# Splitting the first two context tiles of the next batch on ScalarE and VectorE as well as on GpSimd

## The chip, the cores and the metric

The kernel runs on one core of one Trainium2 chip. The metric is the device time of one execution in microseconds (us). Lower is better. The core has TensorE (matmuls; PE in the profile, its weight loads PEld), VectorE (DVE), ScalarE (ACT), GpSimd (POOL) and SyncE (SP), which here issues transfers. The engines run on their own and wait for each other through semaphores; each takes its instructions strictly in the order in which they are written.

## The reference, cut to what matters

The program is a chain of six layers on x (8 batches of 64 rows, 512 wide). The first is a cross attention to a context of 1601 rows per batch, with 32 query heads that share 8 heads of keys and values:

```python
q = (query @ Wq + bq).reshape(B, L, NKV, G, HDIM)       # 8, 64, 8, 4, 128
k_, v_ = jnp.split(kv @ Wkv + bkv, 2, axis=-1)          # kv: 8 x 1601 x 512
scores = jnp.einsum('blkgd,bmkd->bkglm', q, k) * scale
attn = jax.nn.softmax(scores, axis=-1)
o = jnp.einsum('bkglm,bmkd->blkgd', attn, v)
```

Behind it come a state space layer, a ternary linear layer, a second attention to the context, a self attention and a gated feed-forward layer. The change touches only the first attention.

## The kernel before

**The split.** TensorE's matmuls work on rounded operands (fp32r). To keep precision each operand is held as a high part (the value rounded by a copy) and a low part (the raw value minus the high part, the residue), and a product is three matmuls: high by high, high by low, low by high (the helper `product`, L59 to L61). So every operand must be split before TensorE can use it.

**The context.** For a batch the context lies in SBUF transposed, with the 512 features as four chunks of 128 partitions by 1602 columns, as `ctx_hi` and `ctx_lo`. It is loaded and split in four tiles (TILES) of 402, 402, 402 and 396 columns, so a tile is 128 partitions by 4 x 402 = 1608 elements. Raw tiles come into `ctx_raw`, which has two slots: tiles 0 and 2 share one, tiles 1 and 3 the other. `Context.split` does one tile on GpSimd: L110 the high part, L114 the low part (L109 and L113 do one padding column of the last tile). `hi_set` and `lo_set` count the tiles done; in the attention they are `ctx_hi_set` and `ctx_lo_set`.

**The work of one head** (index j = 0 to 7 in batch b). TensorE computes the scores against the key tiles that it made before (`scores`), the key tiles of the next head (`key_tile`, four tiles, 12 matmuls each), the attention of the head before (`attend`) and, after every even head, the values of this head and the next (`value_tile`, six tiles g = 0 to 5 of 256 context rows, 24 matmuls each). Key and value tiles go through `kv_ps`, two banks of PSUM in turn: ScalarE copies the high part out, VectorE then makes the residue (L855, L862) and counts `kv_free`, and the tile after the next may begin. ScalarE also copies the scores out, does the exponentials and the high parts of the probabilities; VectorE the maxima, the shifts and the sums; GpSimd the low parts of the probabilities (`low`, L504, L508, L511), the split of one row of sums (`sum_low`, L533, L536) and of the weights and queries that come next.

**The change of batch** comes seven times. In group j = 6 (NKV - 2) TensorE makes the last value tiles from the old context, and GpSimd, after `low` and `sum_low` of head 6, runs `split_ctx`: for each tile it waits until it has landed and until the value tiles that read the same columns are done, and splits it. Then follow the weights. SyncE loads the raw tiles 0 and 1 of the next batch long before, at j = 2. Tiles 2 and 3 it loads in group j = 6, each when the low part of the tile in the same slot is done:

```python
if j == NKV - 2 and not last:
    for t in range(2, NT):
        sp.wait_ge(ctx_lo_set, b * NT + NT + t - 1)
        context.load(sp, b + 1, t)
```

TensorE, in group j = 7, computes scores and attention and then the key tiles of head 0 of the next batch; there each key tile t waits for the low part of context tile t:

```python
if j % NKV == 0:
    at = b + j // NKV
    pe.wait_ge(ctx_lo_set, at * NT + t + 1)
```

The order on each engine is written out by hand in its `group` function, below. `drive` runs the groups of all heads and batches.

Of the kernel before, what the change touches and what calls it, by code (L numbers as in the profile page):

```python
# [7 lines left out]
F32 = mybir.dt.float32  # L8
F32R = mybir.dt.float32r
ACT = mybir.ActivationFunctionType  # L10
AX_X = mybir.AxisListType.X
AX_XY = mybir.AxisListType.XY
P = 128
# [37 lines left out]
def apart(eng, passed):  # L51


    eng.sem_inc(passed, 1)
# [214 lines left out]
def cross_attention(nc, context, early, rest, output, s_ps, st, wk, wv, ident, q_dram, o_dram):  # L269

    B, _, KC, S = context.ctx_t.shape
# [28 lines left out]
    def value_at(j):  # L300

        return key_at(j - j % 2) + 2 * NT
# [15 lines left out]
    def has_keys(j, last):  # L318

        return not (last and j == NKV - 1)  # L320

    with Scope(nc, "xa") as sc:
# [62 lines left out]
        def d_ps(j, alone=False):  # L385
            if alone:
                return m_ps[:, 0, :]
            return o_ps[:, j % 2, NQ:2 * NQ]

        def free_before(b, j, g):  # L390

            if g < NSLOT:
                return unit(b, j) * NG + (NSLOT, 1, 2)[g]
            return unit(b, j) * NG + g + 1
# [72 lines left out]
        def _(pool):  # L467
# [23 lines left out]

            def split_ctx(b, n):

                for t, (c, w) in enumerate(TILES):
                    pool.wait_ge(ctx_in[t], (n + 1) * 16)
                    used = min(NV, -(-(c + w) // (2 * P)))
                    pool.wait_ge(kv_full, b * KV_TILES + value_at(NKV - 2) + used)
                    apart(pool, passed)
                    context.split(pool, t, n * NT + t + 1)

# [214 lines left out]
        @block.scalar  # L715
        def _(act):
            def key_tile(b, j, t):
                c, w = TILES[t]
                n = key_at(j) + t
                act.wait_ge(kv_full, b * KV_TILES + n + 1)  # L720
                nc.scalar.activation(k_hi[:, c:c + w], kv_ps[:, n % 2, 0:w], ACT.Identity,  # L721
                                     bias=bk_sb[:, j % NKV:j % NKV + 1]).then_inc(kv_hi, 1)

            def value_tile(b, j, g):
                n = value_at(j) + g
                act.wait_ge(kv_full, b * KV_TILES + n + 1)
                nc.scalar.activation(v_hi[:, 2 * g:2 * g + 2, :], kv_ps[:, n % 2, :].rearrange("p (c d) -> p c d", c=2),  # L727
                                     ACT.Copy).then_inc(kv_hi, 1)

            def copies(b, j, start, until):  # L730
                for g in range(start, until):
                    m = min(2, NC - 2 * g)
                    r = rows(2 * g)
                    act.wait_ge(s_full, unit(b, j) * NG + g + 1)
                    nc.scalar.activation(st[0:r, j % 2, g, :, 0:m].rearrange("p q c -> p c q"),  # L735
                                         s_ps[0:r, g % NSLOT, 0:m * NQ].rearrange("p (c q) -> p c q", c=m),
                                         ACT.Copy).then_inc(s_free, 1)

            def diagonal(b, j):
                act.wait_ge(nmx_set, unit(b, j) + 1)  # L740
                for u in range(NU):
                    end = nc.scalar.activation(diag[:, u * P:(u + 1) * P], ident[:, :], ACT.Copy, scale=nmx[:, u:u + 1])
                end.then_inc(diag_set, 1)

            def exponential(b, j, p):
                t = scored(j, p)
                act.wait_ge(sub_set, unit(b, j) * NP + p + 1)
                nc.scalar.activation(t, t, ACT.Exp, scale=SCALE).then_inc(exp_set, 1)  # L748

            def high(b, j, p):  # L750
                act.wait_ge(exp_set, unit(b, j) * NP + p + 1)
                act.wait_ge(o_full, unit(b, j) + 1)
                if p == NP - 1:
                    nc.scalar.activation(pt_rest[0:ROWS, :, :],
                                         rest_scores(j, 0, ROWS).unsqueeze(1).broadcast_to([ROWS, 2, NQ]),
                                         ACT.Copy).then_inc(hi_set, 1)
                    return
                nc.scalar.activation(by_chunk(pt_hi, p), scored(j, p).rearrange("p g q c -> p g c q"),  # L758
                                     ACT.Copy).then_inc(hi_set, 1)

            def upper_sums(b, j):
                act.wait_ge(sum_set, unit(b, j) + 1)
                nc.scalar.activation(upper[:, :], sums[HP:P, 1, :], ACT.Copy).then_inc(upper_set, 1)

            def with_bias(b, j):
                act.wait_ge(on_set, unit(b, j) + 3)
                nc.scalar.activation(o_sb[:, j % 2], o_sb[:, j % 2], ACT.Identity,
                                     bias=bv_sb[:, j:j + 1]).then_inc(o_free, 1)

            def first():  # L770
                act.wait_ge(bias_in, 32)
                for t in range(NT):
                    key_tile(0, 0, t)
                group(0, 0, False, True)

            def first_unit(b, j):

                exponential(b, j, 0)
                exponential(b, j, 1)
                value_tile(b, j, 0)  # L780
                exponential(b, j, 2)
                exponential(b, j, 3)
                high(b, j, 0)
                value_tile(b, j, 1)
                high(b, j, 1)
                high(b, j, 2)
                value_tile(b, j, 2)
                high(b, j, 3)
                upper_sums(b, j)
                for g in range(3, NV):  # L790
                    value_tile(b, j, g)

            def group(b, j, last, alone=False):
                if j % 2 == 0:
                    copies(b, j, 0, NG)
                    if not alone:
                        high(b, j - 1, 0)
                        upper_sums(b, j - 1)
                    key_tile(b, j + 1, 0)
                    if not alone:  # L800
                        high(b, j - 1, 1)
                    key_tile(b, j + 1, 1)
                    if not alone:
                        high(b, j - 1, 2)
                        high(b, j - 1, 3)
                    key_tile(b, j + 1, 2)
                    diagonal(b, j)
                    key_tile(b, j + 1, 3)
                    if alone:
                        first_unit(b, j)  # L810
                        return
                    for p in range(NP):
                        exponential(b, j, p)
                    high(b, j, 0)
                    high(b, j, 1)
                    value_tile(b, j, 0)
                    with_bias(b, j - 1)
                    high(b, j, 2)
                    high(b, j, 3)
                    for g in range(1, NV):  # L820
                        value_tile(b, j, g)
                        if g == 2:
                            upper_sums(b, j)
                elif has_keys(j, last):
                    copies(b, j, 0, NG)
                    diagonal(b, j)
                    key_tile(b, j + 1, 0)
                    with_bias(b, j - 1)
                    exponential(b, j, 0)
                    key_tile(b, j + 1, 1)  # L830
                    exponential(b, j, 1)
                    key_tile(b, j + 1, 2)
                    exponential(b, j, 2)
                    exponential(b, j, 3)
                    key_tile(b, j + 1, 3)
                else:
                    copies(b, j, 0, NG)
                    diagonal(b, j)
                    for p in range(NP):
                        exponential(b, j, p)  # L840
                        high(b, j, p)
                    upper_sums(b, j)
                    act.wait_ge(kv_full, B * KV_TILES)
                    output.second_high(act)
                    with_bias(b, j - 1)

            drive(act, first, group, lambda b: with_bias(b, NKV - 1))

        @block.vector
        def _(dve):  # L850
# [59 lines left out]
            def summed_in_two(b, j, h):  # L910
# [6 lines left out]
                else:  # L917
# [4 lines left out]
                    nc.vector.tensor_tensor(sums[:, 1, :], sums[:, 0, :], m_ps[:, 1, :], ALU.add).then_inc(sum_main, 1)  # L922
                    with_rest(b, j)

            def folded(b, j):
                dve.wait_ge(upper_set, unit(b, j) + 1)
                nc.vector.tensor_tensor(upper[:, :], sums[0:HP, 1, :], upper[:, :], ALU.add).then_inc(fold_set, 1)
# [33 lines left out]
            def group(b, j, last, alone=False):  # L961
                if j % 2 == 0:
# [20 lines left out]
                    for g in range(2, NV):  # L983
                        value_tile(b, j, g)
                        if g == 2:
                            folded(b, j)
                    return
                maxima(b, j, 0)
                maxima(b, j, 1)
# [2673 lines left out]
```

## Time and profile before

| | |
|---|---|
| median of 3 runs | 2604.21 us (2603.81 to 2615.51) |
| profiled execution | 2602.36 us |
| its span, from the first to the last instruction | 2600.6 us |
| TensorE matmuls busy | 2480.7 us |
| VectorE busy | 1844.5 us |
| ScalarE busy | 1503.5 us |
| GpSimd busy | 1499.0 us |
| mean granted clock of TensorE, as a share of full speed | 0.982 |

The first attention takes the stretch from about 130 to 1870 us. "Busy" counts the time in which an instruction ran. A wait is put down to the instruction whose end released it. Times in a timeline are microseconds from the start of the span.

### The profile page before, as it was taken

The numbers are of one execution on the slowest core, as the hardware profiler recorded it, in microseconds if no ns is written. First come the engines' busy times: TensorE is split into PE (matmuls) and PEld (weight loads), VectorE is DVE, ScalarE is ACT, GpSimd is POOL, SyncE is SP. The second block draws the span as 40 slices with busy tenths as digits, with TensorE's granted clock in tenths as the row PEclk, the third lists the DMA queues.
The fourth block names the chain that finished last, engine by engine and source line by source line (L and its number), as shares of the span: only waits on it lengthen the run. The fifth ranks groups of instructions, "written<-read, shape, count | busy, mean of one in ns | idle before, by whom it ended". The sixth has DMA issues, their size and how long they took to land. (4 is left out here: it accounts for less than half of the span.)

```text
span 2600.6 us, 42754 instructions
## 1 busy us (share of the span) xinstructions
PE 2480.7 (95%) x16984; PEld 2271.7 (87%) x16984; DVE 1844.5 (71%) x2078; ACT 1503.5 (58%) x2591; POOL 1499.0 (58%) x1222
## 2 busy tenths in 40 slices
PE   8999999999999999999999999999999699989889
PEld 6899999999999999999999999999977477754557
DVE  4158777778777787777877777777756699843473
ACT  3356656666665666556665566666643577622672
POOL 3345696586668569657666855966510499400352
PEclk9999999999999999999999999999999799999889
DMA  6511111121101201102110121110261300188200
GB/s 222 191 59 54 30 59 54 35 66 54 37 22 60 73 29 60 55 29 65 62 31 28 60 66 35 54 37 28 74 217 53 130 1 1 53 295 310 97 1 17
DMA packets 112239, 188.72 MB, mean 73 GB/s; under 512 B 9940, under 2 KB 74836, under 8 KB 110252
## 3 DMA queue, kind: packets, MB, share of 16 engines
q1 hardware_dynamic: 103724, 177.64, 20.4%
q10 hardware_dynamic: 8320, 8.39, 0.9%
q8 instruction: 133, 2.18, 0.4%
q14 instruction: 62, 0.51, 0.1%
HBM read 165.98 MB, written 20.02 MB: 72 GB/s over the span
## 5 line engine op out<-in xcount | busy, mean ns | idle before, releaser
L504 POOL TENSOR_TENSOR xa_pt_lo<-xs_st,xa_pt_hi 128x1024 fp32r<-128x1024 f32 x191 | 468.2, 2480 | 454.4 <-ACT xa_pt_hi L758 454.4
L59 PE MATMUL ctx_kv_ps<-ctx_wv_hi,ctx_hi 128*128 128x256 f32 x1536 | 431.7, 281 | 1.8 <-DVE xa_v_lo L862 1.8
L60 PE MATMUL ctx_kv_ps<-ctx_wv_lo,ctx_hi 128*128 128x256 f32 x1536 | 430.0, 280 | 0.0
L61 PE MATMUL ctx_kv_ps<-ctx_wv_hi,ctx_lo 128*128 128x256 f32 x1536 | 429.9, 280 | 0.0
L59 PE MATMUL ctx_kv_ps<-ctx_hi,ctx_wk_hi 128*128 128x402 f32 (+1 forms) x1024 | 360.1, 352 | 21.2 <-POOL ctx_lo L114 19.4
L60 PE MATMUL ctx_kv_ps<-ctx_lo,ctx_wk_hi 128*128 128x402 f32 (+1 forms) x1024 | 354.2, 346 | 0.0
L61 PE MATMUL ctx_kv_ps<-ctx_hi,ctx_wk_lo 128*128 128x402 f32 (+1 forms) x1024 | 354.2, 346 | 0.0
L59 PEld LDWEIGHTS ctx_kv_ps<-ctx_wv_hi,ctx_hi 128*128 128x128 f32 x1536 | 288.6, 188 | 2.2 <-DVE xa_v_lo L862 2.2
L60 PEld LDWEIGHTS ctx_kv_ps<-ctx_wv_lo,ctx_hi 128*128 128x128 f32 x1536 | 289.4, 188 | 0.0
L61 PEld LDWEIGHTS ctx_kv_ps<-ctx_wv_hi,ctx_lo 128*128 128x128 f32 x1536 | 288.5, 188 | 0.0
L735 ACT ACTIVATE xs_st<-xs_s_ps 128x512 f32<-128x512 f32 (+1 forms) x448 | 262.9, 603 | 29.5
L748 ACT ACTIVATE xs_st<-xs_st 128x1024 f32<-128x1024 f32 (+1 forms) x256 | 228.1, 903 | 64.8 <-DVE xs_st L896 56.7
L896 DVE TENSOR_TENSOR xs_st<-xs_st,xa_m_ps 128x1024 f32<-128x1024 f32 (+1 forms) x256 | 253.8, 1013 | 5.9 <-PE xa_m_ps L635 2.7
L727 ACT ACTIVATE xa_v_hi<-ctx_kv_ps 128x512 fp32r<-128x512 f32 x192 | 114.8, 598 | 245.2 <-PE ctx_kv_ps L61 245.2
L855 DVE SCALAR_TENSOR_TENSOR xa_k_lo<-ctx_kv_ps,ctx_bk_sb,xa_k_hi 128x402 fp32r<-128x402 f32 (+1 forms) x256 | 161.9, 633 | 123.7 <-ACT xa_k_hi L721 123.7
L862 DVE TENSOR_TENSOR xa_v_lo<-ctx_kv_ps,xa_v_hi 128x512 fp32r<-128x512 f32 x192 | 131.8, 686 | 158.0 <-ACT xa_v_hi L727 158.0
L721 ACT ACTIVATE xa_k_hi<-ctx_kv_ps,ctx_bk_sb 128x402 fp32r<-128x402 f32 (+1 forms) x256 | 152.5, 596 | 156.8 <-PE ctx_kv_ps L61 149.8
L61 PE MATMUL xs_s_ps<-xa_q_hi,xa_k_lo 128*128 128x256 f32 (+1 forms) x832 | 234.7, 282 | 0.0
L59 PE MATMUL xs_s_ps<-xa_q_hi,xa_k_hi 128*128 128x256 f32 (+1 forms) x832 | 233.6, 281 | 0.0
L60 PE MATMUL xs_s_ps<-xa_q_lo,xa_k_hi 128*128 128x256 f32 (+1 forms) x832 | 233.1, 280 | 0.0
L867 DVE TENSOR_REDUCE xa_m_ps<-xs_st 128x256 f32<-128x1536 f32 (+1 forms) x97 | 188.2, 1940 | 53.0 <-ACT xs_st L735 48.9
L59 PE MATMUL xa_o_ps<-xa_pt_hi,xa_v_hi 128*128 128x256 f32 x768 | 216.9, 282 | 0.8 <-DVE xa_pt_lo L931 0.8
(528 smaller groups left out, 6761.9 us busy)
## 6 DMA issues: line engine op xcount, KB each, us to landing
ctx_raw<-in_ctx_t SPq DMA_DIRECT2D x24, 804.0 KB, 6.7
ctx_wk_raw<-in_xa_wk SPq DMA_DIRECT2D x64, 256.0 KB, 2.8
ctx_wv_raw<-in_xa_wv SPq DMA_DIRECT2D x32, 512.0 KB, 4.3
n_back<-in_ctx SPq DMA_DIRECT2D x8, 1280.0 KB, 10.3
q_raw<-in_xa_wq SPq DMA_DIRECT2D x8, 1024.0 KB, 5.0
q_scratch<-q_q_sb ACTq DMA_DIRECT2D x8, 1024.0 KB, 4.4
ctx_q_raw<-q_scratch SPq DMA_DIRECT2D x64, 128.0 KB, 2.7
o_scratch<-xa_o_sb SPq DMA_DIRECT2D x64, 128.0 KB, 1.7
```

The source lines that it names most:

```text
L59: nc.tensor.matmul(out, left[0], right[0], start=first, stop=False)
L60: nc.tensor.matmul(out, left[0], right[1], start=False, stop=False)
L61: return nc.tensor.matmul(out, left[1], right[0], start=False, stop=last)
L504: nc.gpsimd.tensor_tensor(by_chunk(pt_lo, p), scored(j, p).rearrange("p g q c -> p g c q"), by_chunk(pt_hi, p).bitcast(F32), ALU.subtract) ...
L721: nc.scalar.activation(k_hi[:, c:c + w], kv_ps[:, n % 2, 0:w], ACT.Identity, bias=bk_sb[:, j % NKV:j % NKV + 1]).then_inc(kv_hi, 1)
L727: nc.scalar.activation(v_hi[:, 2 * g:2 * g + 2, :], kv_ps[:, n % 2, :].rearrange("p (c d) -> p c d", c=2), ACT.Copy).then_inc(kv_hi, 1)
L735: nc.scalar.activation(st[0:r, j % 2, g, :, 0:m].rearrange("p q c -> p c q"), s_ps[0:r, g % NSLOT, 0:m * NQ].rearrange("p (c q) -> p c q", ...
L748: nc.scalar.activation(t, t, ACT.Exp, scale=SCALE).then_inc(exp_set, 1)
L855: nc.vector.scalar_tensor_tensor(out=k_lo[:, c:c + w], in0=kv_ps[:, n % 2, 0:w], scalar=bk_sb[:, j % NKV:j % NKV + 1], in1=k_hi[:, c:c + w ...
L862: nc.vector.tensor_tensor(v_lo[:, 2 * g:2 * g + 2, :], kv_ps[:, n % 2, :].rearrange("p (c d) -> p c d", c=2), v_hi[:, 2 * g:2 * g + 2, :]. ...
L867: return nc.vector.tensor_reduce(out, st[:, j % 2, a:z, :, :].rearrange("p g q c -> p q g c"), AX_XY, op)
L896: nc.vector.tensor_tensor(t, t, m_ps[0:r, 1, :].unsqueeze(1).unsqueeze(3).broadcast_to([r, g, q, m]), ALU.add).then_inc(sub_set, 1)
```

## The change

At a change of batch, the split of tiles 2 and 3 stays as it was, and the steps of tiles 0 and 1 are shared out. ScalarE makes the high part of tile 0 after value tile 2 (and the copy of the upper sums), and the high part of tile 1 after value tile 4. VectorE makes the low part of tile 0 after value tile 3. GpSimd makes the low part of tile 1 as the first step of `split_ctx`, when both high parts and the low part of tile 0 are done, and then splits tiles 2 and 3 as before. The waits for the value tiles that read the same columns go with the high parts. The loads and what they wait for are not changed.

```diff
--- before.py
+++ after.py
@@ -386,6 +386,11 @@
             if alone:
                 return m_ps[:, 0, :]
             return o_ps[:, j % 2, NQ:2 * NQ]
+
+        def values_used(b, t):
+
+            c, w = TILES[t]
+            return b * KV_TILES + value_at(NKV - 2) + min(NV, -(-(c + w) // (2 * P)))
 
         def free_before(b, j, g):
 
@@ -491,10 +496,14 @@
 
             def split_ctx(b, n):
 
-                for t, (c, w) in enumerate(TILES):
+                pool.wait_ge(ctx_hi_set, n * NT + 2)
+                pool.wait_ge(ctx_lo_set, n * NT + 1)
+                apart(pool, passed)
+                raw, hi, lo = context.parts(1)
+                nc.gpsimd.tensor_tensor(lo, raw, hi.bitcast(F32), ALU.subtract).then_inc(ctx_lo_set, 1)
+                for t in range(2, NT):
                     pool.wait_ge(ctx_in[t], (n + 1) * 16)
-                    used = min(NV, -(-(c + w) // (2 * P)))
-                    pool.wait_ge(kv_full, b * KV_TILES + value_at(NKV - 2) + used)
+                    pool.wait_ge(kv_full, values_used(b, t))
                     apart(pool, passed)
                     context.split(pool, t, n * NT + t + 1)
 
@@ -757,6 +766,13 @@
                     return
                 nc.scalar.activation(by_chunk(pt_hi, p), scored(j, p).rearrange("p g q c -> p g c q"),
                                      ACT.Copy).then_inc(hi_set, 1)
+
+            def context_high(b, t):
+                n = b + 1
+                act.wait_ge(ctx_in[t], (n + 1) * 16)
+                act.wait_ge(kv_full, values_used(b, t))
+                raw, hi, _ = context.parts(t)
+                nc.scalar.activation(hi, raw, ACT.Copy).then_inc(ctx_hi_set, 1)
 
             def upper_sums(b, j):
                 act.wait_ge(sum_set, unit(b, j) + 1)
@@ -821,6 +837,8 @@
                         value_tile(b, j, g)
                         if g == 2:
                             upper_sums(b, j)
+                        if j == NKV - 2 and not last and g in (2, 4):
+                            context_high(b, g // 2 - 1)
                 elif has_keys(j, last):
                     copies(b, j, 0, NG)
                     diagonal(b, j)
@@ -921,6 +939,11 @@
                         dve.wait_ge(sum_lo_set, n)
                     nc.vector.tensor_tensor(sums[:, 1, :], sums[:, 0, :], m_ps[:, 1, :], ALU.add).then_inc(sum_main, 1)
                     with_rest(b, j)
+
+            def context_low(b, t):
+                dve.wait_ge(ctx_hi_set, (b + 1) * NT + t + 1)
+                raw, hi, lo = context.parts(t)
+                nc.vector.tensor_tensor(lo, raw, hi.bitcast(F32), ALU.subtract).then_inc(ctx_lo_set, 1)
 
             def folded(b, j):
                 dve.wait_ge(upper_set, unit(b, j) + 1)
@@ -984,6 +1007,8 @@
                         value_tile(b, j, g)
                         if g == 2:
                             folded(b, j)
+                        if j == NKV - 2 and not last and g == 3:
+                            context_low(b, 0)
                     return
                 maxima(b, j, 0)
                 maxima(b, j, 1)
```

## Rows read from the trace of the kernel before

**Rows 1.** The page: busy time, share of the span and instructions of the engines.
```profile
PE 2480.7 (95%) x16984; PEld 2271.7 (87%) x16984; DVE 1844.5 (71%) x2078; ACT 1503.5 (58%) x2591; POOL 1499.0 (58%) x1222
```

**Rows 2.** Who TensorE waited for, 130 to 1870 us: total, times, longest.
```profile
PE ctx_kv_ps L59 <- POOL ctx_lo L114: 19.4, 14, 2.4
```

**Rows 3.** Timeline of GpSimd, L533 once per head: start, us, instruction.
```profile
226.35 0.40 POOL L533 TENSOR_SCALAR xa_sum_halves<-xa_upper 64x256 fp32r<-64x256 f32 x1
...
280.16 0.40 POOL L533 TENSOR_SCALAR xa_sum_halves<-xa_upper 64x256 fp32r<-64x256 f32 x1
...
333.93 0.40 POOL L533 TENSOR_SCALAR xa_sum_halves<-xa_upper 64x256 fp32r<-64x256 f32 x1
...
392.37 0.40 POOL L533 TENSOR_SCALAR xa_sum_halves<-xa_upper 64x256 fp32r<-64x256 f32 x1
...
1757.06 0.40 POOL L533 TENSOR_SCALAR xa_sum_halves<-xa_upper 64x256 fp32r<-64x256 f32 x1
```

**Rows 4.** Timeline of GpSimd around the first change of batch.
```profile
324.69 7.44 POOL L504 TENSOR_TENSOR xa_pt_lo<-xs_st,xa_pt_hi 128x1024 fp32r<-128x1024 f32 x3
...
334.42 0.73 POOL L536 TENSOR_TENSOR xa_sum_halves<-xa_upper,xa_sum_halves 64x256 fp32r<-64x256 f32 x1
...
335.37 1.54 POOL L110 TENSOR_SCALAR ctx_hi<-ctx_raw 128x1608 fp32r<-128x1608 f32 x1 [0.23 <-POOL xa_sum_halves L536]
...
337.00 3.68 POOL L114 TENSOR_TENSOR ctx_lo<-ctx_raw,ctx_hi 128x1608 fp32r<-128x1608 f32 x1
...
345.71 1.53 POOL L110 TENSOR_SCALAR ctx_hi<-ctx_raw 128x1608 fp32r<-128x1608 f32 x1 [0.42 <-DMA ctx_raw<-in_ctx_t]
...
352.88 2.98 POOL L114 TENSOR_TENSOR ctx_lo<-ctx_raw,ctx_hi 128x1580 fp32r<-128x1580 f32 x1
```

**Rows 5.** Timeline of SyncE's queue: the two loads of tiles 2 and 3 merged.
```profile
340.70 5.20 SPq L93 DMA_DIRECT2D ctx_raw<-in_ctx_t  x2
```

**Rows 6.** Timeline of TensorE around the first change, single matmuls.
```profile
333.76 0.28 PE L59 MATMUL ctx_kv_ps<-ctx_wv_hi,ctx_hi 128*128 128x256 f32 x1
...
341.20 0.28 PE L59 MATMUL xa_o_ps<-xa_pt_hi,xa_v_hi 128*128 128x256 f32 x1
...
348.40 0.35 PE L59 MATMUL ctx_kv_ps<-ctx_hi,ctx_wk_hi 128*128 128x402 f32 x1
...
350.44 0.35 PE L61 MATMUL ctx_kv_ps<-ctx_hi,ctx_wk_lo 128*128 128x402 f32 x1
...
355.92 0.70 PE L59 MATMUL ctx_kv_ps<-ctx_hi,ctx_wk_hi 128*128 128x396 f32 x1 [2.41 <-POOL ctx_lo L114]
```

**Rows 7.** Busy times, 356 to 360 us; behind POOL: granted clock, DMA share.
```profile
356.00:360.00 4.00, 4.00 (x15) 4.00 (x16) 0.00 (x0) 0.14 (x1) 3.83 (x3) 0.60 0.02 4
```

**Rows 8.** Groups of ScalarE by shape, SBUF to SBUF: busy us, mean ns.
```profile
L1643 ACT ACTIVATE mp_w_hi<-ahead_raw 128x1024 fp32r<-128x1024 f32 x7 | 7.4, 1052 | 2.5 <-POOL mp_xpad L1586 2.5
...
L1345 ACT ACTIVATE q_w_hi<-q_raw 128x2048 fp32r<-128x2048 f32 x7 | 13.4, 1918 | 9.9 <-DMA v_scratch<-q_q_sb 5.5 <-ACT q_q_sb L1318 4.4
```

**Rows 9.** Groups of VectorE by shape, two SBUF inputs: busy us, mean ns.
```profile
L1696 DVE TENSOR_TENSOR mp_w_lo<-ahead_raw,mp_w_hi 128x1024 fp32r<-128x1024 f32 x7 | 8.6, 1222 | 3.7 <-ACT mp_w_hi L1643 3.7
...
L1375 DVE TENSOR_TENSOR q_w_lo<-q_raw,q_w_hi 128x2048 fp32r<-128x2048 f32 x7 | 17.8, 2538 | 54.3 <-ACT q_w_hi L1345 54.3
```

**Rows 10.** Timeline of ScalarE in the value tiles of head 6.
```profile
329.87 0.42 ACT L763 ACTIVATE xa_upper<-xa_sums 64x256 f32<-64x256 f32 x1 [0.96 <-DVE xa_sums L901]
...
333.96 0.60 ACT L727 ACTIVATE xa_v_hi<-ctx_kv_ps 128x512 fp32r<-128x512 f32 x1 [2.23 <-PE ctx_kv_ps L61]
```

**Rows 11.** Timeline of VectorE in the value tiles of head 6.
```profile
330.36 2.05 DVE L927 TENSOR_TENSOR xa_upper<-xa_sums,xa_upper 64x256 f32<-64x256 f32 x1
...
332.34 0.67 DVE L862 TENSOR_TENSOR xa_v_lo<-ctx_kv_ps,xa_v_hi 128x512 fp32r<-128x512 f32 x1
```

**Rows 12.** Spread of the fold (ns), and of the loads of the context.
```profile
L927 DVE TENSOR_TENSOR xa_upper<-xa_sums,xa_upper x64: 403/1432/2066, 169.3 to 1890.6; 64x256 f32<-64x256 f32 x64
...
DMA to landing us min/median/max: 4.8/6.2/11.7
```

## The prediction

> **What bounds the kernel now.** I read four views, in this order. First the page's busy times: TensorE's matmuls are busy for 95% of the span [rows 1], so a change to other engines can save only time in which TensorE stands still, or runs at a lower clock. Second, who TensorE waited for, in the stretch of the first attention: the largest sum there is 14 waits on the low part of a context tile, 19.4 us [rows 2]. There are seven changes of batch, so each has two such waits. Third, how long a pair of heads lasts. The reader is to take one GpSimd instruction that comes once per head, L533, as a clock: a pair inside a batch takes 280.16 - 226.35 = 53.81 us, the pair across the first change of batch 392.37 - 333.93 = 58.44 [rows 3]. From 226.35 to 1757.06 there are 28 pairs, seven of them across a change: 1530.71 - 28 x 53.80 (53.81 rounded down to the mean of several pairs) = 24.3 us is what all seven cost beyond their work, and it is the most that this change can give back there. The first costs 4.6, the other six 19.7 together, 3.3 each. Fourth, the timelines around the first change, to see what is late.
>
> The late thing is a chain, not GpSimd's load. The split of tile 2 needs a raw buffer that tile 0 frees. GpSimd starts tile 0 at 335.37, when it has finished head 6, and ends its low part at 340.68 (337.00 + 3.68); SyncE issues the load of tile 2 at 340.70 [rows 4, 5]. It has landed when GpSimd goes on at 345.71, 5.0 us later. High and low of tiles 2 and 3 then take until 352.88 + 2.98 = 355.86. So the last low part comes 15.16 us after that load is issued, and TensorE's key tile 3 starts at 355.92 [rows 4, 6]. Without the waits: tile 1 starts at 348.40, its twelfth matmul at 350.44, so twelve take 2.22 us and tiles 2 and 3 could start at 350.62 and 352.84 [rows 6]. Tile 3's lateness is 3.0 us; the small wait on tile 2 is inside it. At the first change TensorE then ran at a granted clock of 0.60 as a mean over 4 us, between the levels of 1.2 and 2.4 GHz, after standing still [rows 7]; that is the 4.6 against 3.3.
>
> **The change part by part.** ScalarE gets two copies of 128x1608. Rows of the same kind take 1052 ns at 1024 columns and 1918 at 2048 [rows 8]; in proportion between them, 1.55 us. VectorE gets one subtraction of two SBUF tiles: 1222 ns at 1024 and 2538 at 2048 [rows 9], so 1.97 us. The bounds are the rows at either size. GpSimd loses two high parts and one low part, 1.5 + 3.7 + 1.5 us. No transfer is added; two are issued at other times.
>
> *High part of tile 0.* It stands behind the upper sums, which end at 329.87 + 0.42 = 330.29 [rows 10]. So it runs 330.3 to 331.9. Its raw data was loaded four heads earlier, and the value tiles that used its columns are done. Behind it on ScalarE is the copy of value tile 3. Before the change it comes one value tile before the one at 333.96, and a value tile lasts 2.83 us (24 matmuls; from 333.76 to 341.20 TensorE issues 63 of this size, the tile and 39 of scores, one each 0.118 us [rows 6]): so at 331.13. After it, it runs from 331.9 to 332.5. Behind that is VectorE's residue of the same tile, now at 332.34 because a fold of sums runs before it [rows 11]; then 332.5 to 333.2. TensorE needs that bank at 333.76, for value tile 5 [rows 6]. It is hidden with 0.5 us to spare; with the 2048-column row, 1.92 us, there is still 0.1 us. Without that cover each microsecond would cost 7 us.
>
> *Low part of tile 0.* It starts at 333.2 at the earliest. Unhindered it ends at 335.2. It may have to wait for GpSimd: the fold L927, 256 columns wide, took 2.05 us from 330.36 and ended 0.3 us after GpSimd's train of three (324.69 + 7.44 = 332.13), while 1024 columns take 1.22 elsewhere [rows 9, 11, 4]. GpSimd's next train for head 6 ends with L536 at 334.42 + 0.73 = 335.15 [rows 4]. Behind all of it the low part ends at 335.15 + 1.97 = 337.1. I take this worse end, and keep 335.2 as the other. Behind it on VectorE stand the residues of value tiles 4 and 5, 0.7 us each, then done by 338.5. TensorE wants tile 5's when the scores of head 7 are over, at 341.20 [rows 6]: hidden, 2.7 us to spare.
>
> *The load of tile 2* is issued at 337.1 instead of 340.70, and lands at 342.1.
>
> *High part of tile 1* follows the copy of value tile 4 (333.96 + 0.60) [rows 10]: 334.6 to 336.1, before the next copy, which is due 2.83 us after 333.96. *Low part of tile 1* on GpSimd waits for both: it starts at 337.1 and ends at 340.8, with 3.68 from tile 0's row. Then the load of tile 3 goes out, 5.0 us, landed at 345.8. GpSimd needs it after tile 2: 342.1 + 5.3 = 347.4 (tile 0's split took 340.68 - 335.37 = 5.3). It is in time.
>
> *Tile 3's low part* ends 15.16 us after the issue of tile 2's load: 337.1 + 15.16 = 352.3, against the 352.84 at which TensorE gets there. Tile 2's ends at 347.4, against 350.62. Both waits go, with 0.6 us left in the worse case and 2.5 in the better. The break points follow from this. Nothing is gained if the load still goes out at 340.70, and all of it once it goes out by 352.84 - 15.16 = 337.68. The other six changes cost 3.3 us rather than 3.0, so their margin is narrower by 0.3.
>
> What is late next is nothing that I find: without the waits a pair across a change is a pair like the others, where GpSimd, ScalarE and VectorE keep up, and GpSimd comes out of the split earlier. So the sum is seven changes, 24.3 us, with the lower clock of the first in it.
>
> One rule bears on the low part. The Trainium skill (SBUF — State Buffer, "Who interferes with whom") says that a VectorE instruction with two SBUF inputs and a GpSimd instruction that reads SBUF exclude each other, and the one that comes second waits for the whole of the other. By that rule, the trace agrees: L927 ended just behind a GpSimd instruction. By it the low part would wait out one instruction and not the train, and the load would go out near 335.8; the sum stays.
>
> **The rivals.** *A: the chain moves too little (0.10).* VectorE's low part and GpSimd's train hold each other up longer, or the first load takes the 6.2 us that is this transfer's median [rows 12] rather than 5.0. Then tile 3's low part comes at up to 353.5 and TensorE waits 0.7 to 1.5 us a change with its restarts: 5 to 10 us come back, 2583 to 2588. For it speaks that the margin is 0.3 to 0.6 us; against it that it was computed with the worse end. *B: no change (0.05).* The load goes out at 340 anyway, because something holds VectorE for 3 us more; 2602. GpSimd's longest single instruction there is 3.7 us, but none that long runs before 335.4. *C: slower (0.03), the exclusion between VectorE and GpSimd.* The low part must end after 340.70, 5.5 us past its unhindered end, before a microsecond is lost; for 0.5% it must be after 342.6 (13 us are 1.9 us a change), and then value tile 5's residue is late for 341.20 too. It would give 2615 or more. Against it: on all 64 heads the fold L927 never took over 2.07 us [rows 12]. *D: the copies stall value tile 5,* needing more than 0.5 us beyond 1.55: 1 us of it would take back 3.5 us. Both bounding rows exclude it; it counts in A.
>
> **How the numbers follow.** The profiled execution took 2602.36 us, its span is 2600.6. 2602.36 - 24.3 = 2578.1. The median of the three runs is 2604.21, 1.85 above the profiled one; I put the forecast between, at 2579. Later stages have their own stretches at the lower clock, and work that comes 24 us earlier may meet them otherwise: at the first change such a stretch cost 1.3 us, so four of them either way make 5 us. Range of the forecast: 2573 to 2585 (chance 0.82). With A's 2588 and the scatter of the median the range is 2573 to 2590. 0.5% is 13 us, about what a measurement of this kernel can tell from no change; faster by more than that is below 2591. The forecast and A give 0.92 less a little for A's tail: faster 0.91, same 0.06, slower 0.03.
>
> **What the profile of the changed kernel would show.** Right: no waits of TensorE for the low part of the context; L533 53.8 us apart per pair across a change too; the load of tile 2 issued some 3.6 to 5 us earlier, seen from value tile 5; copies of 128x1608 at 1.5 to 1.6 us on ScalarE, the subtraction on VectorE at 1.9 to 4 us, its excess being the wait for GpSimd; no clock drop at the first change. Wrong: waits of TensorE on a value tile's residue (D), a load issued later than 337.7 in the first change's terms (A, B), or a subtraction of over 4 us (C).

## The result

The changed kernel takes 2577.99 us (median of 4 runs, 2576.86 to 2579.10) against 2607.77 us for the kernel before (4 runs, 2603.81 to 2615.51): the ratio is 0.9882, with a 95% interval from 0.9855 to 0.9909. A second measurement gave 2579.32 against 2605.72 us, a ratio of 0.9902 (0.9886 to 0.9917); it is told below with the other runs. The forecast was 2579 us. The profiled execution took 2577.61 us, with a span of 2575.7 us.

The page of the changed kernel gives this for the engines:

```profile
PE 2475.4 (96%) x16984; PEld 2271.0 (88%) x16984; DVE 1857.3 (72%) x2085; ACT 1525.6 (59%) x2605; POOL 1464.5 (57%) x1201
```

Against [rows 1] GpSimd is busy for 34.5 us less, ScalarE for 22 and VectorE for 13 us more. TensorE is busy for 95 to 96% in both, and that hides where the time came from. Who TensorE waited for in the first attention shows it (total, times, longest):

```profile
PE xa_m_ps L648 <- POOL xa_sum_halves L545: 2.9, 1, 2.9
PE ctx_kv_ps L59 <- DVE xa_k_lo L873: 1.8, 1, 1.8
```

The row on the low part of the context, 19.4 us in 14 waits [rows 2], is gone, and no other took its place. None of the waits left stands at a change of batch. The two largest are shown: the first comes at 1866.6 us, behind the last head, and in the kernel before the same wait (2.9 us) comes at 1892.9, outside of the stretch; the second has the same 1.8 us in the kernel before. GpSimd's instruction that comes once per head is L542 here:

```profile
224.42 0.40 POOL L542 TENSOR_SCALAR xa_sum_halves<-xa_upper 64x256 fp32r<-64x256 f32 x1
...
278.22 0.40 POOL L542 TENSOR_SCALAR xa_sum_halves<-xa_upper 64x256 fp32r<-64x256 f32 x1
...
333.61 0.40 POOL L542 TENSOR_SCALAR xa_sum_halves<-xa_upper 64x256 fp32r<-64x256 f32 x1
...
385.81 0.40 POOL L542 TENSOR_SCALAR xa_sum_halves<-xa_upper 64x256 fp32r<-64x256 f32 x1
...
1730.76 0.40 POOL L542 TENSOR_SCALAR xa_sum_halves<-xa_upper 64x256 fp32r<-64x256 f32 x1
```

A pair inside a batch takes 53.80 us as before. From 224.42 to 1730.76, the same 28 pairs as in [rows 3], are 1506.34 us, against 28 x 53.80 = 1506.4: nothing is left of what the seven changes of batch cost. The stretch shrank by 1530.71 - 1506.34 = 24.37 us. The pair up to 333.61 takes 55.39 and the one behind it 52.20, because this GpSimd instruction comes 1.6 us late at head 6; what holds it is shown next. The span shrank by 24.9 us. The stretch ahead of 224.42 is 1.9 us shorter and the one behind 1730.76 1.4 us longer (844.9 against 843.5 us), neither of which the change touches; two of the kernels below, which differ from the changed one only at the changes of batch, have their first mark at 226.05.

Around the first change of batch GpSimd's timeline reads:

```profile
331.21 2.31 POOL L520 TENSOR_TENSOR xa_pt_rest<-xs_st,xa_pt_rest 1x256 fp32r<-1x256 f32 x1
...
335.04 3.04 POOL L503 TENSOR_TENSOR ctx_lo<-ctx_raw,ctx_hi 128x1608 fp32r<-128x1608 f32 x1 [0.20 <-POOL xa_sum_halves L545]
338.47 1.54 POOL L110 TENSOR_SCALAR ctx_hi<-ctx_raw 128x1608 fp32r<-128x1608 f32 x1 [0.40 <-issue]
...
345.66 2.99 POOL L114 TENSOR_TENSOR ctx_lo<-ctx_raw,ctx_hi 128x1580 fp32r<-128x1580 f32 x1
```

SyncE's queue, where the two loads of tiles 2 and 3 are merged:

```profile
332.94 5.75 SPq L93 DMA_DIRECT2D ctx_raw<-in_ctx_t  x2
```

ScalarE and VectorE in the value tiles of head 6:

```profile
328.40 1.56 ACT L775 ACTIVATE ctx_hi<-ctx_raw 128x1608 fp32r<-128x1608 f32 x1
329.86 0.58 ACT L736 ACTIVATE xa_v_hi<-ctx_kv_ps 128x512 fp32r<-128x512 f32 x1
...
332.50 1.55 ACT L775 ACTIVATE ctx_hi<-ctx_raw 128x1608 fp32r<-128x1608 f32 x1
```

```profile
328.45 2.08 DVE L950 TENSOR_TENSOR xa_upper<-xa_sums,xa_upper 64x256 f32<-64x256 f32 x1
330.47 0.69 DVE L880 TENSOR_TENSOR xa_v_lo<-ctx_kv_ps,xa_v_hi 128x512 fp32r<-128x512 f32 x1
331.08 1.83 DVE L946 TENSOR_TENSOR ctx_lo<-ctx_raw,ctx_hi 128x1608 fp32r<-128x1608 f32 x1
332.82 0.69 DVE L880 TENSOR_TENSOR xa_v_lo<-ctx_kv_ps,xa_v_hi 128x512 fp32r<-128x512 f32 x1
```

And TensorE, at value tile 5 and at key tile 3 of the next batch:

```profile
331.80 0.28 PE L59 MATMUL ctx_kv_ps<-ctx_wv_hi,ctx_hi 128*128 128x256 f32 x1
...
350.87 0.34 PE L59 MATMUL ctx_kv_ps<-ctx_hi,ctx_wk_hi 128*128 128x396 f32 x1
```

Everything here is 1.96 us earlier than in the kernel before (331.80 against 333.76 [rows 6]); add that to compare. VectorE's low part of tile 0 ends at 331.08 + 1.83 = 332.91, the load of tile 2 goes out at 332.94 (334.9 in the old time, instead of 340.70), and the last low part ends at 345.66 + 2.99 = 348.65. TensorE gets to key tile 3 at 350.87. It has 2.2 us to spare where it was 3.0 us short. The last low part comes 15.7 us after the load is issued here, where it was 15.16: GpSimd is busy with tile 1 up to 338.08 and goes on with tile 2 at 338.47, 5.5 us after the issue instead of 5.0. No matmul there is marked with a wait. Over 354 to 358 us, which is the stretch of [rows 7] in this kernel's time, the granted clock (the first of the last three columns) is whole, where it had been 0.60:

```profile
354.00:358.00 4.00, 4.00 (x35) 4.00 (x34) 3.97 (x3) 3.66 (x6) 1.25 (x3) 1.00 0.27 102
```

### The profile page after: what moved, and what is told of

Read it like the earlier page. It is cut to its first block and busy times, and to the rows that moved or that the text cites. A ratio compares the mean times of both kernels' runs of the same rounds, so it can differ in the third digit from the quotient of the medians.

```text
span 2575.7 us, 42761 instructions
## 1 busy us (share of the span) xinstructions
PE 2475.4 (96%) x16984; PEld 2271.0 (88%) x16984; DVE 1857.3 (72%) x2085; ACT 1525.6 (59%) x2605; POOL 1464.5 (57%) x1201
```

## The experiments

The theory under test has two deadlines. The last low part of the split comes 15.2 us after tile 2's load is issued, or when GpSimd's own steps are through, whichever is later; it costs time only past TensorE's arrival. Rival 1 counts only GpSimd's work, rival 2 only the time of the load. The expectations call them so. Each kernel is compared with runs of the kernel before on the same chip.

### The changed kernel again

The changed kernel itself, measured once more.

> The changed kernel once more, beside the kernel before in five rounds: 0.5 closer than the first measurement. The pairs of heads gave 24.4 us, so a ratio of 0.9906 if nothing else differs; the first measurement had 0.9882 with an interval from 0.9855 to 0.9909. Every theory says the same; it tells how much of the 29.8 us between the two medians is scatter of the kernel before.

Measured: 2579.32 us (2575.97 to 2581.86, 5 runs) against 2605.72, ratio 0.9902 (0.9886 to 0.9917). The kernel before scatters by 10 us between runs, the changed one by 6. The 24.4 us of the pairs, a ratio of 0.9906, lie in both intervals. The rest of the first difference is scatter. It goes with the mean granted clock of an execution: of the kernel before, 2600.66 us had 0.983 and 2610.42 had 0.979; of the changed kernel, 2575.97 had 0.983 and 2581.86 had 0.980.

### Tile 0 alone is shared out

```diff
 # split_ctx, GpSimd
-pool.wait_ge(ctx_hi_set, n * NT + 2)
+pool.wait_ge(ctx_hi_set, n * NT + 1)
 pool.wait_ge(ctx_lo_set, n * NT + 1)
-apart(pool, passed)
-raw, hi, lo = context.parts(1)
-nc.gpsimd.tensor_tensor(lo, raw, hi.bitcast(F32), ALU.subtract).then_inc(ctx_lo_set, 1)
-for t in range(2, NT):
+for t in range(1, NT):
 # group, ScalarE
-if j == NKV - 2 and not last and g in (2, 4):
-    context_high(b, g // 2 - 1)
+if j == NKV - 2 and not last and g == 2:
+    context_high(b, 0)
```

> The change without its second copy: ScalarE makes only the high part of tile 0, VectorE its low part, and GpSimd splits tiles 1, 2 and 3 whole. Theory (two deadlines: the last low part comes 15.2 us after tile 2's load is issued or when GpSimd's own steps are through, whichever is later, and costs time only past TensorE's arrival at key tile 3, 350.87 in the changed kernel's trace): the load goes out as in the changed kernel, near 332.9; GpSimd goes from 335.0 through 1.5 + 3.0 + 5.3 + 4.9 us and ends near 350.2. So 0.6 us to spare, no waits, 2578 us (2576 to 2582). Rival 1 (what counts is how much work GpSimd is rid of: 5.2 instead of 6.8 us, a gain in proportion): 2584. Rival 2 (only the time of the load counts): 2578 too.

Measured: 2579.00 us (2577.01 to 2581.05) against 2601.97, ratio 0.9909 (0.9893 to 0.9926). TensorE has no wait for the low part. GpSimd's steps at the first change:

```profile
334.97 1.54 POOL L110 TENSOR_SCALAR ctx_hi<-ctx_raw 128x1608 fp32r<-128x1608 f32 x1 [0.23 <-PE ctx_kv_ps L61]
...
339.59 1.55 POOL L110 TENSOR_SCALAR ctx_hi<-ctx_raw 128x1608 fp32r<-128x1608 f32 x1
...
346.79 2.99 POOL L114 TENSOR_TENSOR ctx_lo<-ctx_raw,ctx_hi 128x1580 fp32r<-128x1580 f32 x1
```

It ends at 349.78, 1.1 us before TensorE gets there. The forecast was 350.2; the terms that it names add up to 349.7. So the second copy on ScalarE bought 1.1 us of margin and no time. A gain in proportion to GpSimd's lost work, rival 1 in its simple form, would have been 2584 us, which is outside of the runs.

### The high parts alone are moved

```diff
 # split_ctx, GpSimd
-pool.wait_ge(ctx_hi_set, n * NT + 2)
-pool.wait_ge(ctx_lo_set, n * NT + 1)
-apart(pool, passed)
-raw, hi, lo = context.parts(1)
-nc.gpsimd.tensor_tensor(lo, raw, hi.bitcast(F32), ALU.subtract).then_inc(ctx_lo_set, 1)
+for t in range(2):
+    pool.wait_ge(ctx_hi_set, n * NT + t + 1)
+    apart(pool, passed)
+    raw, hi, lo = context.parts(t)
+    nc.gpsimd.tensor_tensor(lo, raw, hi.bitcast(F32), ALU.subtract).then_inc(ctx_lo_set, 1)
 for t in range(2, NT):
 # group, VectorE
-if j == NKV - 2 and not last and g == 3:
-    context_low(b, 0)
```

> The change without VectorE's part: ScalarE makes both high parts, GpSimd both low parts and tiles 2 and 3. Theory of two deadlines: GpSimd makes the low part of tile 0 from about 333.5 to 337, the load of tile 2 goes out there, the last low part comes 15.2 us later, near 351.7 to 352.2; TensorE waits 0.8 to 1.3 us for it, 1.1 to 1.7 with the restart, at each of seven changes: 2586 to 2590 us. Rival 1 (GpSimd's work: 3.1 of 6.8 us less): by its sum alone it would end near 351.0, 2578 to 2581 us. Rival 2 (the load alone): as the theory, 2586 to 2590.

Measured: 2590.14 us (2586.29 to 2592.22) against 2601.97, ratio 0.9950 (0.9933 to 0.9966). The timeline of GpSimd, then the loads of tiles 2 and 3 (merged), then the waits of TensorE:

```profile
332.80 0.74 POOL L520 TENSOR_TENSOR xa_pt_rest<-xs_st,xa_pt_rest 1x256 fp32r<-1x256 f32 x1
...
335.06 6.67 POOL L503 TENSOR_TENSOR ctx_lo<-ctx_raw,ctx_hi 128x1608 fp32r<-128x1608 f32 x2 [0.20 <-POOL xa_sum_halves L545]
343.80 1.53 POOL L110 TENSOR_SCALAR ctx_hi<-ctx_raw 128x1608 fp32r<-128x1608 f32 x1 [2.07 <-DMA ctx_raw<-in_ctx_t]
...
350.97 2.99 POOL L114 TENSOR_TENSOR ctx_lo<-ctx_raw,ctx_hi 128x1580 fp32r<-128x1580 f32 x1
```

```profile
338.76 3.57 SPq L93 DMA_DIRECT2D ctx_raw<-in_ctx_t  x2
```

```profile
PE ctx_kv_ps L59 <- POOL ctx_lo L114: 9.2, 7, 1.5
```

GpSimd is through with tile 1 at 341.7 and then idles for 2.07 us until tile 2 has landed. The last low part ends at 353.96, 15.2 us after the load. This run's times are 1.6 us later than the changed kernel's, so TensorE wants it at 352.5. Without the 2.07 us of idle time it would have been there at 351.9. GpSimd's own work is not what is late: the load is. Rival 1 fails. Seven waits of 1.3 us as a mean cost 10.8 us of pairs (1743.25 - 226.05 = 1517.2 against 1506.4).

### The load of tile 2 is held back

```diff
 # group, SyncE, j == NKV - 2
 for t in range(2, NT):
-    sp.wait_ge(ctx_lo_set, b * NT + NT + t - 1)
+    sp.wait_ge(ctx_lo_set, b * NT + NT + 2)
     context.load(sp, b + 1, t)
```

> The changed kernel, but the load of tile 2 waits for the low part of tile 1 too, so that it goes out near 338.1 instead of 332.9; nobody's work changes. Theory of two deadlines: the last low part near 353.3, 2.4 us late, 2.7 with the restart: 7 x 2.7 = 19 us of the gain go, 2597 us (2594 to 2600). Rival 1 (GpSimd's work): nothing goes, 2578 us. Rival 2 (the load alone): as the theory.

Measured: 2604.05 us (2601.46 to 2607.12, 10 runs) against 2601.97, ratio 1.0006 (0.9996 to 1.0016). GpSimd, with no step more than in the changed kernel, idled for the load:

```profile
338.09 1.27 SPq L93 DMA_DIRECT2D ctx_raw<-in_ctx_t  x2
```

```profile
343.42 1.53 POOL L110 TENSOR_SCALAR ctx_hi<-ctx_raw 128x1608 fp32r<-128x1608 f32 x1 [5.35 <-DMA ctx_raw<-in_ctx_t]
...
350.59 2.98 POOL L114 TENSOR_TENSOR ctx_lo<-ctx_raw,ctx_hi 128x1580 fp32r<-128x1580 f32 x1
```

The last low part came at 353.57, 0.3 us from the forecast. That part of the theory holds, but the time is 7 us above what it gave. At the second and the sixth change the load also took longer to land (6.2 us instead of 5.3), and TensorE waited there for tile 2 as well, 0.8 us each time: nine waits in seven changes. GpSimd at the second change, then the waits of TensorE:

```profile
563.81 1.54 POOL L110 TENSOR_SCALAR ctx_hi<-ctx_raw 128x1608 fp32r<-128x1608 f32 x1 [6.24 <-DMA ctx_raw<-in_ctx_t]
```

```profile
PE ctx_kv_ps L59 <- POOL ctx_lo L114: 17.9, 9, 2.4
```

These two waits are worth about 2 us. The next run shows where the rest is from.

### Work is given back to GpSimd, and not to the load

```diff
 # split_ctx, GpSimd
 raw, hi, lo = context.parts(1)
+nc.gpsimd.tensor_scalar(lo, raw, 1.0, 1.0, ALU.mult, ALU.mult).then_inc(extra, 1)
+pool.wait_ge(extra, 2 * n - 1)
+nc.gpsimd.tensor_tensor(lo, raw, hi.bitcast(F32), ALU.subtract).then_inc(extra, 1)
+pool.wait_ge(extra, 2 * n)
 nc.gpsimd.tensor_tensor(lo, raw, hi.bitcast(F32), ALU.subtract).then_inc(ctx_lo_set, 1)
```

> The changed kernel, with work given back to GpSimd and not to the load: it makes the low part of tile 1 with one copy and one subtraction more (1.5 + 3.0 us, same result), after the load of tile 2 has been issued as early as before. Theory of two deadlines: the last low part near 353.1, 2.2 us late, 2.5 with the restart: 17 us of the gain go, 2595 us (2592 to 2598). Rival 1 (GpSimd's work): the same. Rival 2 (only the time of the load counts): nothing goes, 2578 us.

Measured: 2601.36 us (2599.62 to 2605.19, 10 runs) against 2601.97, ratio 1.0000 (0.9990 to 1.0009). The load of tile 2 went out as early as in the changed kernel, and the whole gain is gone. Rival 2 fails. GpSimd does not idle between its steps of the split, and ends at 352.92 (forecast 353.1):

```profile
332.90 10.51 SPq L93 DMA_DIRECT2D ctx_raw<-in_ctx_t  x2
```

```profile
335.02 1.55 POOL L504 TENSOR_SCALAR ctx_lo<-ctx_raw 128x1608 fp32r<-128x1608 f32 x1 [0.23 <-POOL xa_sum_halves L550]
336.65 3.04 POOL L506 TENSOR_TENSOR ctx_lo<-ctx_raw,ctx_hi 128x1608 fp32r<-128x1608 f32 x1
339.77 3.04 POOL L508 TENSOR_TENSOR ctx_lo<-ctx_raw,ctx_hi 128x1608 fp32r<-128x1608 f32 x1
...
349.93 2.99 POOL L114 TENSOR_TENSOR ctx_lo<-ctx_raw,ctx_hi 128x1580 fp32r<-128x1580 f32 x1
```

The stalls are as long as expected, but the time lost is larger. Two changes of batch side by side tell why. First TensorE's first matmul after the stall at each, and the granted clock of 10 us around it (the last three columns are the clock, the DMA share and GB/s):

```profile
352.98 0.65 PE L59 MATMUL ctx_kv_ps<-ctx_hi,ctx_wk_hi 128*128 128x396 f32 x1 [1.95 <-POOL ctx_lo L114]
...
571.89 0.45 PE L59 MATMUL ctx_kv_ps<-ctx_hi,ctx_wk_hi 128*128 128x396 f32 x1 [1.94 <-POOL ctx_lo L114]
```

```profile
350.00:360.00 10.00, 8.05 (x46) 7.72 (x45) 4.60 (x6) 5.29 (x9) 9.29 (x7) 0.83 0.34 105
...
568.00:578.00 10.00, 8.06 (x56) 7.73 (x55) 6.14 (x7) 6.68 (x11) 9.67 (x9) 1.00 0.37 108
```

And the length of two pairs of heads, one ahead of the change and one across it:

```profile
278.23 0.40 POOL L547 TENSOR_SCALAR xa_sum_halves<-xa_upper 64x256 fp32r<-64x256 f32 x1
...
389.55 0.40 POOL L547 TENSOR_SCALAR xa_sum_halves<-xa_upper 64x256 fp32r<-64x256 f32 x1
...
497.13 0.40 POOL L547 TENSOR_SCALAR xa_sum_halves<-xa_upper 64x256 fp32r<-64x256 f32 x1
...
606.92 0.40 POOL L547 TENSOR_SCALAR xa_sum_halves<-xa_upper 64x256 fp32r<-64x256 f32 x1
```

The two stalls last 1.95 and 1.94 us. After the first the clock fell (from 2.4 to 1.2 GHz for some 3 us, so that 10 us have a mean of 0.83), and the matmul took 0.65 us instead of 0.45. 389.55 - 278.23 = 111.32 us is 3.7 more than two undisturbed pairs (107.60); 606.92 - 497.13 = 109.79 is 2.2 more. So a stall costs 2.2 us, near the 2.5 expected, and another 1.5 where the clock falls. It fell at five of the seven changes: 7 x 2.2 + 5 x 1.5 = 22.9, and the pairs from 224.43 to 1753.77 have 1529.34 - 1506.4 = 22.9. In the run with the late load it also fell at five, and the excess of its pairs, 27.8 us (1758.58 - 224.40 = 1534.18), is made up of the stalls, the two small waits and these falls. In the profiled execution of the kernel before, whose stalls were longer than here (2.4 us), it fell only at the first. Each of these counts is from one execution.

### VectorE's step placed one step earlier

```diff
 # group, VectorE
-if j == NKV - 2 and not last and g == 3:
+if j == NKV - 2 and not last and g == 2:
     context_low(b, 0)
```

> The changed kernel, with VectorE's low part of tile 0 before the residue of value tile 3 instead of behind it. The prediction gave that residue 0.5 us to spare. In the changed kernel's trace the fold ends at 330.53 and GpSimd holds a step until 331.14, so the low part runs to 332.4 at the best and 333.0 at the worst, the residue to 333.1 to 333.7, and TensorE wants the bank at 331.80 for value tile 5: a stall of 1.3 to 1.9 us, 1.5 to 2.1 with the restart, seven times: 10 to 15 us, 2588 to 2593; up to 10 us more if the stalls bring the lower clock, as they did in most changes of the two runs e3_late_load and e4_extra_gpsimd. Rival (VectorE's place doesn't matter, since only the load and GpSimd count, and the load goes out as early): 2578.

Measured: 2587.84 us (2583.54 to 2588.75) against 2605.72, ratio 0.9929 (0.9912 to 0.9947). VectorE and GpSimd, then the stall that TensorE has at value tile 5 (this run's times are 1.6 us later than the changed kernel's):

```profile
332.07 1.82 DVE L946 TENSOR_TENSOR ctx_lo<-ctx_raw,ctx_hi 128x1608 fp32r<-128x1608 f32 x1
333.81 1.27 DVE L880 TENSOR_TENSOR xa_v_lo<-ctx_kv_ps,xa_v_hi 128x512 fp32r<-128x512 f32 x2
```

```profile
332.01 2.48 POOL L517 TENSOR_TENSOR xa_pt_rest<-xs_st,xa_pt_rest 64x256 fp32r<-64x256 f32 x1
```

```profile
334.54 0.38 PE L59 MATMUL ctx_kv_ps<-ctx_wv_hi,ctx_hi 128*128 128x256 f32 x1 [0.92 <-DVE xa_v_lo L880]
```

The stall is 0.9 us, and the pairs of all changes together lose 8.2 us (1740.62 - 226.05 = 1514.57). It was expected at 1.3 to 1.9. VectorE did not wait for GpSimd at all: again it was GpSimd's step that took longer (2.48 us, against 0.74 in the changed kernel, where VectorE's subtraction comes later). A stall of this length did not bring the clock down. The residue behind the new step had little time to spare, as the prediction had it; one step earlier, a third of the gain is lost.

### VectorE's step placed one step later

```diff
 # group, VectorE
-if j == NKV - 2 and not last and g == 3:
+if j == NKV - 2 and not last and g == 4:
     context_low(b, 0)
```

> The changed kernel, with VectorE's low part of tile 0 one value tile later, behind the residue of value tile 4. It starts at 333.3 and ends at 335.2 unhindered, at 336.7 behind GpSimd's two steps for the sums. The break point of the prediction (the load of tile 2 issued 15.2 us before TensorE's arrival at key tile 3, 350.87) is 335.7 here. So the last low part comes at 350.4 to 351.9; also GpSimd's low part of tile 1 starts later, at 335.2 to 336.7, which ends the rest at 348.9 to 350.4, in time. Between no wait and 1.0 us late a change: 2578 to 2586 us. Rival (the exclusion costs whole trains of GpSimd): the load later than 338, 2595 us or more.

Measured: 2578.75 us (2577.30 to 2582.59) against 2605.72, ratio 0.9904 (0.9886 to 0.9922), with no wait for the low part. This run's times are 0.9 us later than the changed kernel's. The load went out at 336.00, the last low part ended 15.3 us later, at 351.32, and TensorE arrived at 351.79:

```profile
336.00 3.88 SPq L93 DMA_DIRECT2D ctx_raw<-in_ctx_t  x2
```

```profile
336.24 3.04 POOL L503 TENSOR_TENSOR ctx_lo<-ctx_raw,ctx_hi 128x1608 fp32r<-128x1608 f32 x1 [2.12 <-DVE ctx_lo L946]
341.17 1.54 POOL L110 TENSOR_SCALAR ctx_hi<-ctx_raw 128x1608 fp32r<-128x1608 f32 x1 [1.89 <-DMA ctx_raw<-in_ctx_t]
...
348.34 2.98 POOL L114 TENSOR_TENSOR ctx_lo<-ctx_raw,ctx_hi 128x1580 fp32r<-128x1580 f32 x1
```

```profile
351.79 0.34 PE L59 MATMUL ctx_kv_ps<-ctx_hi,ctx_wk_hi 128*128 128x396 f32 x1
```

0.47 us to spare, and no time lost. The prediction put the break point at a load issued at 337.68 in the time of the kernel before. In that time the load goes out at 337.05 here, without loss, and at 339.1 in the run with the high parts alone, with a stall of 1.3 us. So the break point lies between the two, as predicted; no run fixes it closer. VectorE's step ran in 1.83 us with no GpSimd step beside it, and the mark of head 6 is not late: 332.89 - 279.04 = 53.85 us.

## Why the prediction was right, point by point

- **What bounds the kernel.** Right: TensorE's waits at the changes of batch were the whole gain, 24.4 us in the pairs for 24.3 forecast, the lower clock after the first stall included.
- **"The late thing is a chain, not GpSimd's load."** Half right, and the step of the reasoning that needs mending. The load was one deadline, and the runs with the high parts alone and with the late load show it. But GpSimd's own work was a second one, almost as late: with 4.6 us of work given back and the load early, the gain is gone. The rows of before say so, if read for it: from 335.37 to 355.86 GpSimd waited for only 0.42 us [rows 4], so with any earlier load and the same work it would have ended at 355.44, still 2.6 us after the 352.84 at which TensorE gets there. "All of it once the load goes out by 337.68" holds only if GpSimd is also rid of enough. The change relieved both, so the number came out; that it rid GpSimd of enough was no part of this step of the argument.
- **High parts on ScalarE.** Sized right: 1.56 and 1.55 us for 1.55. The residue of value tile 3 ended at 331.16, 0.64 us before TensorE wanted the bank, for the 0.5 forecast: rival D did not happen either.
- **Low part on VectorE.** 1.83 us for 1.97. The wait for GpSimd, which was taken at its worst end, did not come, and this is the term that the prediction had the wrong way round: VectorE went first, and GpSimd's small step L520 took 2.31 us instead of the 0.74 that it takes in the run without VectorE's step. It ended at 333.52, 0.6 us after VectorE's (332.91), about its own 0.74 us. The same delay moved GpSimd's mark of head 6 by 1.6 us, so that the sign "53.8 us apart per pair across a change" came out as 55.39 and 52.20. The load was to go out 3.6 to 5.5 us earlier by the two bounds; measured, 340.70 - 334.9 = 5.8. The Trainium skill's rule that the second one waits for the whole of the first (SBUF — State Buffer, "Who interferes with whom") fits this row, with GpSimd as the one that waits.
- **The margin** was 2.2 us, near the 2.5 of the better end, by two errors that nearly cancel: the load went out 0.3 us earlier than that end has it, and the last low part came 15.7 us after it instead of 15.16. The run with VectorE's step later shows 0.47 us still to be enough. The fixed 5.0 us for the load is the weaker term: in the run with the late load GpSimd could go on with tile 2 5.3 us after the issue at the first change and 6.2 us after it at the second (563.81, issued at 557.59).
- **The rivals.** A, B and C did not happen. The prediction put the point of no gain at a load issued at 340.70 in the old time; in the run with the late load it went out at 340.0, and the ratio is 1.0006. That nothing is left there, 0.7 us before that point, comes mostly from the falls of the clock. No kernel came out slower by more than the measurement can tell.
- **What was left out.** Each stall was priced by its length and one drop of the clock in seven. The two runs that brought stalls of 2 us and more back had five drops in seven, some 1.5 us each, and came out 6 to 7 us above what was expected. It didn't touch the forecast, which has no stalls.

## What to carry to other kernels

A wait that ends a chain of transfers and of work on one engine has two deadlines; compute both from the idle time inside the chain before moving work. Moving what relieves only one gains no more than the distance to the other, and here the two were 0.42 us apart. One copy and one subtraction of tile 0 give everything, because that tile frees the buffer for the next load and its split is 5 us of GpSimd's work; the second copy is only margin. Where a step is slipped into another engine's order matters by the slack of what stands behind it: one place earlier cost 8 us.

## What the runs showed of the hardware

The granted clock after a stall cannot be told from the stall's length alone. In one profiled execution each, stalls of 1.92 to 1.96 us brought a fall at five of seven changes of batch; stalls of 2.4 us at one of seven in the kernel before; stalls of 2.1 to 2.4 us at five of seven in the run with the late load; and stalls of up to 1.5 us (the runs with the high parts alone and with VectorE's step earlier) at none. The seven stalls of 1.92 to 1.96 us stand in the same place of the program and are alike, and still two of them brought no fall. A fall cost 1.5 us in that run and 1.3 to 1.7 in the others. What decides it stays open. The same kernel's executions also differ: the kernel before, measured beside the changed one, took from 2600.66 us at a mean clock of 0.983 to 2610.42 at 0.979, so the count in one execution need not be that of the next.

When VectorE's subtraction of two SBUF tiles of 128x1608 met a row of short GpSimd steps, it was GpSimd that waited. In all three placements the subtraction took 1.82 to 1.83 us, also where no GpSimd step ran beside it. The GpSimd step that began just before or behind its start took 2.31 us instead of 0.74 in one placement and 2.48 instead of 0.74 in another.
